# Attention scores as four row-tiled matmuls of 32 partitions, keys spread over 4 copies instead of 16, in a four-layer transformer kernel

## What is computed

```python
s = jnp.einsum('blhd,bmhd->bhlm', q, k)
if causal:
    s = jnp.where(mask, s, -jnp.inf)
p = jax.nn.softmax(s, axis=-1)
return jnp.einsum('bhlm,bmhd->blhd', p, v)
```

## Time and profile before

| | us |
|---|---|
| median of 3 runs | 4222.94 (4222.19 to 4223.15) |
| the profiled execution | 4218.46 |
| its span | 4216.7 |
| TensorE matmuls busy | 4112.9 |
| TensorE weight loads busy | 2922.2 |
| VectorE busy | 2716.3 |
| ScalarE busy | 2733.6 |
| GpSimd busy | 1597.5 |

### The profile page before, as it was taken

How to read it: one execution, slowest core, us unless ns; L and a number is a source line. 1 busy time by engine, 2 the same in 40 slices (tenths; PEclk the granted TensorE clock), 3 DMA queues, 4 the chain that set the end, 5 groups by cost and what they waited for, 6 DMA issues and landing times.

```text
span 4216.7 us, 87546 instructions
## 1 busy us (share of the span) xinstructions
PE 4112.9 (98%) x32576; PEld 2922.2 (69%) x32576; DVE 2716.3 (64%) x5914; ACT 2733.6 (65%) x4850; POOL 1597.5 (38%) x1316
## 2 busy tenths in 40 slices
PE   7999999999999999999999999999999999999998
PEld 4666677776667777777766767777776666777775
DVE  7766555567776655556787765655677776555565
ACT  4677766556667776655666777665566677666555
POOL 4444322234553432124455433223344543321233
PEclk9999999999999999999999999999999999999999
DMA  1000011000000001110000000101000000011000
GB/s 60 1 3 23 13 43 39 33 29 1 17 9 3 23 13 42 41 41 19 10 9 9 3 23 23 43 31 41 19 10 10 9 3 23 24 41 41 31 14 9
DMA packets 52621, 92.60 MB, mean 22 GB/s; under 512 B 11817, under 2 KB 35313, under 8 KB 51953
## 3 DMA queue, kind: packets, MB, share of 16 engines
q1 hardware_dynamic: 52208, 87.01, 6.3%
HBM read 82.80 MB, written 4.19 MB: 21 GB/s over the span
## 4 chain that ended last, share of the span: by engine, by line
PE 87%; DVE 6%; ACT 3%; DMA 1%; POOL 1%; issue 1%; SPq 0%; POOLq 0%; ACTq 0%; DVEq 0%
PE ps L952 19%; PE ps L965 14%; PE ps L1034 11%; PE ps L1042 10%; PE ps L977 8%; PE ps L985 3%; PE ps L926 3%; PE ps L997 2%; PE ps L955 2%; PE ps L935 2%; PE ps L910 2%; PE ps L1002 1%; PE ps L1091 1%; PE ps L1061 1%; DVE mx L1342 1%
## 5 line engine op out<-in xcount | busy, mean ns | idle before, releaser
L1531 POOL TENSOR_TENSOR kx<-kT,k_sb 128x616 f32<-128x616 f32 (+1 forms) x704 | 1038.4, 1475 | 1191.9 <-PE ps L952 621.5
L952 PE MATMUL ps<-kx,qT 128*128 128x308 f32 (+1 forms) x2816 | 1067.7, 488 | 16.4 <-DVE pr L1348 7.1
L1342 DVE TENSOR_REDUCE mx<-ps 128x8 f32<-128x616 f32 (+1 forms) x704 | 671.7, 954 | 603.8 <-PE ps L952 341.5
L1190 ACT ACTIVATE pt<-ps 77x512 f32<-77x512 f32 (+1 forms) x1408 | 776.3, 591 | 268.1 <-PE ps L965 265.3
L1181 ACT ACTIVATE pr<-pr 128x616 f32<-128x616 f32 (+1 forms) x704 | 588.0, 837 | 359.5 <-DVE pr L1348 354.7
L965 PE MATMUL ps<-k_sb,pr 128*77 128x128 f32 (+1 forms) x5632 | 783.9, 277 | 2.4 <-ACT og L1199 1.5
L965 PEld LDWEIGHTS ps<-k_sb,pr 128*77 128x77 f32 (+1 forms) x5632 | 630.8, 145 | 168.7 <-issue 141.8
L1348 DVE TENSOR_TENSOR pr<-ps,mx 128x616 f32<-128x616 f32 (+1 forms) x704 | 671.5, 954 | 24.2
L952 PEld LDWEIGHTS ps<-kx,qT 128*128 128x128 f32 x2816 | 477.7, 190 | 253.0 <-issue 174.9
L1034 PE MATMUL ps<-hT,ew 128*128 128x512 f32 x1024 | 452.4, 594 | 3.7 <-DMA ew<-weights 3.6
L977 PE MATMUL ps<-pt,v 77*16 77x128 f32 (+2 forms) x11264 | 428.5, 275 | 2.7 <-ACT pt L1190 2.7
(11 more groups left out here) (168 smaller groups left out, 5076.9 us busy)
## 6 DMA issues: line engine op xcount, KB each, us to landing
ew<-weights SPq DMA_DIRECT2D x128, 512.0 KB, 4.7
x<-x SPq DMA_DIRECT2D x16, 256.0 KB, 3.2
out<-xh SPq DMA_DIRECT2D x16, 256.0 KB, 2.4
cT<-ctx_cols SPq DMA_DIRECT2D x16, 154.0 KB, 3.2
qT<-mask_pairs SPq DMA_DIRECT2D x16, 154.0 KB, 3.3
kx<-ctx_rows SPq DMA_DIRECT2D x16, 154.0 KB
w_sb<-weights SPq DMA_DIRECT2D x1, 1542.0 KB, 7.5
w_sb<-weights SPq DMA_DIRECT2D x1, 1280.0 KB
```

The lines of the kernel that those rows point to most:

```text
L952: i = mm(o, qT[s][:, b * L:(b + 1) * L], k[:, 4 * j * keys:4 * (j + 1) * keys], start=True, stop=mask is None)
L1190: go_act(pt[s][0:keys, q % 2, :], p[0:keys, :], ACT.Copy).then_inc(probsT_ready.sem, 1)
L1342: link(v_.tensor_reduce(m, tile, AX.X, ALU.max, negate=True))
L1531: tell(pool, g_.tensor_tensor(dst, kT[s][:, b * keys:(b + 1) * keys].unsqueeze(1).broadcast_to([128, 8, keys]), masks.unsqueeze(2).broadca ...
```

## The change

- `scores` becomes one step for a whole batch. It writes `heads // 4` banks: four row tiles of 32 partitions for 16 heads, two of 64 partitions for 8 heads. Tile `g` contracts only its own 32 (or 64) partitions, which hold heads 4g to 4g+3. The masks are put into the banks first.
- `spread` becomes one step for a batch with 4 copies of the keys: copy `j` keeps, in each group, the rows of head `j` of that group (`in_tile`, two small reductions made once). `kx` has four slots of `4 * keys` columns per stream in the same memory.
- The softmax is a step of its own, `soft`, once per half, and each half releases its own pair of banks.
- The planner: costs in `parts` changed for nearly all steps, `LATE` (a delay after TensorE and ScalarE) added, `HOP` from 0.15 to 0.1, another choice among free banks, any adjacent pair instead of four fixed ones, and new values of `LEAD`, `PHASES`, `STAY` and `EAGER`. So the order of every queue differs.

```diff
-            out += [("spread", a, s, *units[n]), ("scores", a, s, *units[n])]
+            if not units[n][1]:
+                out += [("spread", a, s, units[n][0]), ("scores", a, s, units[n][0])]
+            out.append(("soft", a, s, *units[n]))
...
     if kind == "scores":
-        mask = 0.0 if t.mask is None else 0.3 + 0.0034 * keys
-        return [(P, pe(4 * keys, 2) + mask), (V, 2.55 if t.own else 1.7), (A, act(8 * keys))]
+        tiles = t.heads // 4
+        mask = 0.0 if t.mask is None else tiles * (0.02 + 0.0004 * 4 * keys)
+        return [(P, 0.3 + (0.00182 if tiles == 4 else 0.00182) * 4 * keys + mask)]
+    if kind == "soft":
+        return [(V, 2.52 if t.own else 1.67), (A, act(8 * keys, 0.5))]
...
-            option = min(banks_of(step), key=lambda o: max(bank_free[b] for b in o))
-            clear = max(bank_free[b] for b in option)
-            if clear == FOREVER:
+            free_now = [bank_free[b] + HOP <= t for b in range(8)] + [False]
+
+            def cost(o):
+                clear = max(bank_free[b] for b in o)
+                beside = sum(free_now[b - 1] + free_now[b + 1] for b in o)
+                return max(clear + HOP, t), beside, -sum(bank_free[b] for b in o)
+            option = min(banks_of(step), key=cost)
+            if max(bank_free[b] for b in option) == FOREVER:
                 return None
-            t = max(t, clear + HOP)
+            t = cost(option)[0]
...
-LEAD = 2.64378649
-PHASES = (0, 0.270197968, 0.113519094, 0.191236723)
-STAY = 60.9002828
...
+LEAD = 0.416394515
+PHASES = (0, 0.280901424, 0.477195298, 0.528231786)
+STAY = 47.9352789
...
-ANY = [(b,) for b in (7, 6, 5, 4, 3, 2, 1, 0)]
-BANKS = {"scores": [(0, 1), (2, 3), (4, 5), (6, 7)], "rope": [(4, 5), (6, 7), (0, 1), (2, 3)]}
...
+ONE = [(b,) for b in range(8)]
+TWO = [(b, b + 1) for b in range(7)]
+FOUR = [a + b for a in TWO for b in TWO if a[1] < b[0] or b[1] < a[0]]
...
+        if step[0] == "soft" and engine == V:
+            pair = 2 * step[4]
+            bank_free.update(dict.fromkeys(banks["scores", *step[1:4]][pair:pair + 2], end))
...
-                    for j in range(2):
-                        o = bank(pl, step, j)[:, 0:4 * keys]
-                        i = mm(o, qT[s][:, b * L:(b + 1) * L], k[:, 4 * j * keys:4 * (j + 1) * keys],
-                               start=True, stop=mask is None)
-                        if mask is not None:
-                            i = mm(o.rearrange("p (h k) -> p h k", h=4), ident16,
-                                   mask.unsqueeze(1).broadcast_to([128, 4, keys]), start=False, stop=True)
+                    tiles = t.heads // 4
+                    outs = [bank(pl, step, g)[:, 0:4 * keys] for g in range(tiles)]
+                    if mask is not None:
+                        for o in outs:
+                            mm(o.rearrange("p (h k) -> p h k", h=4), ident16,
+                               mask.unsqueeze(1).broadcast_to([128, 4, keys]), start=True, stop=False)
+                    high = 128 // tiles
+                    for g, o in enumerate(outs):
+                        r = slice(high * g, high * (g + 1))
+                        i = mm(o, qT[s][r, b * L:(b + 1) * L], spread_keys[s][r, pl.slot(("spread", a, s, b), NB), 0:4 * keys],
+                               start=mask is None, stop=True)
...
+                link(nc.vector.tensor_reduce(in_tile[heads], K(f"heads{heads}").rearrange("p (g j) -> p j g", j=4), AX.X,
+                                             ALU.add))
...
-                    dst = kx[s][:, pl.slot(step, 2), 0:8 * keys].rearrange("p (h k) -> p h k", h=8)
-                    masks = K("heads16")[:, 8 * h:8 * h + 8] if t.heads == 16 else K("heads8")
                     tell(pool, g_.tensor_tensor(
-                        dst, kT[s][:, b * keys:(b + 1) * keys].unsqueeze(1).broadcast_to([128, 8, keys]),
-                        masks.unsqueeze(2).broadcast_to([128, 8, keys]), ALU.mult), keys_spread, *args)
+                        spread_keys[s][:, pl.slot(step, NB), 0:4 * keys].rearrange("p (h k) -> p h k", h=4),
+                        kT[s][:, b * keys:(b + 1) * keys].unsqueeze(1).broadcast_to([128, 4, keys]),
+                        in_tile[t.heads].unsqueeze(2).broadcast_to([128, 4, keys]), ALU.mult), keys_spread, *args)
```

More of the change, by code:

```diff
@@ L200, in act @@
 def act(n, bias=0.0):
-    return 0.165 + 0.00086 * n + 0.1 * bias
+    return 0.06 + 0.00082 * n + 0.1 * bias
 def parts(step):
     kind, n = step[0], NB * L
-    if kind in ("project", "rope", "values", "spread", "scores", "turn", "mix", "regroup", "out"):
+    if kind in ("project", "rope", "values", "spread", "scores", "soft", "turn", "mix", "regroup", "out"):
         t = ATT[step[1]]
@@ L290, in inputs_of @@
     kind, args = step[0], step[1:]
-    if kind in ("project", "rope", "values", "bias", "spread", "scores", "turn", "mix", "regroup", "out"):
+    if kind in ("project", "rope", "values", "bias", "spread", "scores", "soft", "turn", "mix", "regroup", "out"):
         a, s = args[:2]
@@ L304, in inputs_of @@
         if a and of == "k":
-            out.append((parts(step)[1][0], ("spread", a - 1, s, *last), None))
+            out.append((parts(step)[1][0], ("spread", a - 1, s, NB - 1), None))
         if a and of == "v":
@@ L327, in inputs_of @@
     if kind == "spread":
+        return [(None, (t.project, a, s, "k"), None)]
+    if kind == "scores":
+        return [(None, ("spread", *args), None), (None, (t.project, a, s, "q"), None)]
+    if kind == "soft":
         n = units.index(args[2:])
[L329 to L333, removed]
+        return ([(None, ("scores", *args[:3]), None)]
                 + ([(V, ("turn", a, s, units[n - 2][0], 2 * units[n - 2][1] + 1), P)] if n >= 2 else []))
@@ L354, in inputs_of @@
     if kind == "context":
-        return [(None, ("scores", 2, s, NB - 1, ATT[2].halves - 1), P)]
+        return [(None, ("scores", 2, s, NB - 1), P)]
     if kind == "fetch":
@@ L426, in ready @@
                 return None
[L427 removed]
+            t = ends[step, chain[k - 1][0]] + LATE[chain[k - 1][0]] + HOP
         else:
@@ L436, in ready @@
                     continue
-                end = ends.get((other, theirs or parts(other)[-1][0]))
-                if end is None:
+                by = theirs or parts(other)[-1][0]
+                if (other, by) not in ends:
                     return None
-                t = max(t, end + HOP)
+                t = max(t, ends[other, by] + LATE[by] + HOP)
         return t
@@ L492, in timetable @@
         if k and chain[k - 1][0] == P and step in banks:
-            bank_free.update(dict.fromkeys(banks[step], end))
+            bank_free.update(dict.fromkeys(banks[step], end + LATE[engine]))
+        if step[0] == "soft" and engine == V:
+            pair = 2 * step[4]
+            bank_free.update(dict.fromkeys(banks["scores", *step[1:4]][pair:pair + 2], end))
         for which, (first, final) in enumerate(SHARED):
@@ L505 @@
 FOREVER = 1e9
-LEAD = 2.64378649
-PHASES = (0, 0.270197968, 0.113519094, 0.191236723)
-STAY = 60.9002828
[L509 to L512, removed]
-ANY = [(b,) for b in (7, 6, 5, 4, 3, 2, 1, 0)]
-BANKS = {"scores": [(0, 1), (2, 3), (4, 5), (6, 7)], "rope": [(4, 5), (6, 7), (0, 1), (2, 3)]}
+LEAD = 0.416394515
+PHASES = (0, 0.280901424, 0.477195298, 0.528231786)
+STAY = 47.9352789
+EAGER = {"load": 1.5, "stats": -0.3, "apply": -0.2, "bias": -4, "spread": 2.7, "scores": 0.3,
+         "bias_mlp": -0.2, "hidden": 0.4, "context": 4.1, "fetch": -4.6, "down": -0.1, "step_size": 16.4,
+         "step_size2": -8.8, "decay_in": -1.8, "decay": 2.6, "weigh": 3.8, "gate_stats": -0.2,
+         "gate_norm": -10.3, "mamba_out": -0.3, "final": -3.9, "store": -3.7}
 WITH_PSUM = ("turn", "mix", "regroup", "norm", "values", "project", "turn_out", "out", "hidden", "mlp", "route", "gates",
@@ L517 @@
              "mamba_out")
+ONE = [(b,) for b in range(8)]
+TWO = [(b, b + 1) for b in range(7)]
+FOUR = [a + b for a in TWO for b in TWO if a[1] < b[0] or b[1] < a[0]]
 def banks_of(step):
-    return BANKS.get(step[0]) or (ANY if step[0] in WITH_PSUM else None)
+    if step[0] == "scores":
+        return FOUR if ATT[step[1]].heads == 16 else TWO
+    return TWO if step[0] == "rope" else ONE if step[0] in WITH_PSUM else None
 class Plan:
@@ L542, in __init__ @@
                 self.before[step] = list(dict.fromkeys(last[b] for b in self.banks[step] if b in last))
-                last.update(dict.fromkeys(self.banks[step], step))
+                for n, b in enumerate(self.banks[step]):
+                    last[b] = ("soft", *step[1:], n // 2) if step[0] == "scores" else step
         self.rank, self.sames = {}, {}
@@ L546, in __init__ @@
             for step in steps:
-                if step[0] in ("spread", "scores", "mix"):
+                if step[0] in ("spread", "soft", "mix"):
                     same = self.sames.setdefault((step[0], step[2] % S), [])
@@ L780, in build @@
```

(2 more changed lines are left out.)

95 lines of the change are left out of this document (49 added, 46 removed).

## The result

The changed kernel takes 4012.92 us (median, 4011.71 to 4015.95) against 4222.74: a ratio of 0.9504, 95% interval 0.9488 to 0.9521. It is 5% faster, and 273 us slower than the forecast of 3740, outside the range of 3600 to 3900. Its profiled execution took 4011.71 us, against 4218.46 before.

A forecast was written before the change was run, and what follows sets the result against it. The prediction took TensorE, busy for 4112.9 of 4216.7 us, as the bound. From 4218.5 us it took 548 for faster score matmuls and added 70 of stalls: 3740 us, range 3600 to 3900.

The forecast's parts named there:

- the term of 548 us: Score matmuls on TensorE: four row tiles run at once, steps of 1.16 and 0.82 us, saving 548 us.
- the extra 0.30: Per score step: 0.20 us for entering and leaving tiled mode, about 0.10 for the first of four loads not overlapped.
- loads one after another: Rival for the score step: row groups load one after another, saving only 404 us, time 3860; chance 0.08.
- staggered pairs: Rival for the score step: eight matmuls need five slots instead of two, saving 255 us, time 3964; chance 0.05.
- no overlap: Rival for the score step: row tiles don't overlap, switching adds 77 us, time 4295, slower; chance 0.05.
- the lighter GpSimd: Spreading on GpSimd falls from 1038 to about 294 us, beside TensorE; no gain booked.
- The stalls that come: Attention-heavy stretches: VectorE holds 87% at most, 65 us of stalls, plus 5 for banks and order: 70 us.
- 74% is all that is shown over 400 us: Argument for the binding engines rival: the trace shows VectorE at most 74% busy over 400 us.
- The rival of binding engines: Attention-heavy stretches: VectorE, ScalarE and banks hold each other up at 80% of VectorE, 215 us, time 3885; chance 0.15.
- The step on the softmax halves: Softmax: scores of both halves hold four banks, second pair 2.45 us longer; mid-size pressure, shown as TensorE idle.
- Its sign of being wrong: On TensorE: idle time over 250 us with waits for the shifted scores (banks) or for ScalarE's copies.

The follow-up runs named there:

- untiled: The changed kernel with each score matmul contracting all 128 partitions instead of its own row tile, order of all queues unchanged: 4466.65 us.
- halves_s: The changed kernel with scores by halves again, two row tiles of 32 partitions into two banks per 8 heads, and its own priorities: 4021.19 us.
- hold: The changed kernel with each half's two banks released only after ScalarE's exponential instead of VectorE's add, order planned anew: 4234.11 us.
- oldparams: The changed kernel with the earlier values of LEAD, PHASES, STAY and EAGER, all steps, costs and bank choice as changed: 4175.18 us.

## Why the prediction was wrong

Right, nearly to the digit, was the term of 548 us. Four at a time, read off the column-tiled mix, held for row tiles; the step with its entry is 1.07 + 0.09 = 1.16 us and 0.74 + 0.09 = 0.83 us, forecast 1.16 and 0.82. Of the extra 0.30, 0.10 us is the second burst's late start: it comes 0.533 us after the first (median of all steps), where untiled matmuls of 512 columns come 0.430 apart. The prediction had that size, but put it on the first of four loads. The rivals of loads one after another, of staggered pairs and of no overlap are all refuted; the four loads start together, so what the Trainium skill says of a load's length (TensorE: Matmul & The Clock Gate, LDWEIGHTS) agrees with the trace (184 ns for 32 rows, 190 for 128) and yet doesn't set the step's length. The Trainium skill's other page (TensorEngine Tiling (Array Packing), Gotcha 1: PSUM Pressure) says that row tiling raises the pressure on PSUM, as different row tiles write to different banks; the trace agrees that the pressure rose, from 17 to 177 us of waits for banks. The prediction used the same page for the drain alone and priced banks and order at 5 us.

Right too: GpSimd (879.0 us, forecast near 850; 318.9 of it the spreading, forecast 294) and VectorE's busy time. That nothing is gained by the lighter GpSimd wasn't tested; before, TensorE waited for its `kx` for 0.8 us in all.

Wrong was the step **The stalls that come**. It measured the new limit by how full VectorE would be in the attention-heavy stretches, 87 to 90%, and gave 5 us to banks and order together. In place of that term of 70 us, 342 came: 160 us more of visible waits for banks, 52 more of other visible idle time, about 48 by the clock and about 80 hidden. The clock, which the prediction had at 1.00 throughout, was in no term of it. The order is mixed into all of these: with nothing changed but priorities the time is 61 us less or 162 more, and the best run of all, with another list and another search, is 3933 us, still above the range. VectorE is busy for 281.7 of the 400 us from 2000 to 2400:

```profile
2000.00:2400.00 400.00, 360.33 (x3464) 247.66 (x3463) 281.67 (x564) 284.27 (x518) 84.63 (x101) 0.98 0.08 24
```

TensorE is still 10% idle there, and VectorE's fullest 400 us have 302.6, 76%. They had 305.8 before: the prediction's "74% is all that is shown over 400 us" missed that stretch. The rival of binding engines named the banks beside VectorE and ScalarE, but priced them by VectorE alone and stopped at 3885. The step on the softmax halves had a good part of the cause (both halves hold four banks, the second 2.45 us longer), called it mid-size and left it 5 us. Its sign of being wrong, TensorE idle over 250 us with waits for the shifted scores, came true at 316.

The method failed in one point: before, TensorE was so full that hardly a wait of it could be seen (17 us for banks), and nothing in that trace gave the banks a price; the prediction should have given them a wide one. The same order with slower score steps shows the effect: in `untiled` TensorE is busier and waits 127 us for banks, in the changed kernel 177.

Open: how much of the hidden 80 us is bank and how much data, what the clock costs by itself (no run held the clock), and how the 342 us divide between banks and order, as each run that changed the hold and let the planner know has another order too.

## What to carry to other kernels

Before pricing a faster step on the busiest engine, add up how long each scarce buffer is held per step and in how many pieces it is taken; a step that is three times faster and takes twice the banks can give a good part of it back. Where the order of all queues is fixed ahead, a relief is to be measured with an order planned for it: 704 releases a microsecond earlier were worth 16 us in the old order and 53 in one planned for them, and that order without the early releases cost 95. A TensorE wait that ends with an instruction whose output the waiting step never reads was here a wait for a bank.

## What was not expected of the hardware

The halving of the clock: with TensorE's idle time up from 104 to 316 us in many small pieces, the mean granted clock fell from 0.998 to 0.978. Over the runs it goes loosely with the idle time: 0.992 with 141 us in `halves_s`, 0.966 with 451 in `hold`, 0.959 with 421 in `oldparams`. Two row tiles take as long as four (1.06 and 1.07 us). And the second burst of a tiled step comes late, the more so the more columns a load has: by 11 ns in the mix with 16 columns a load (0.120 us after the first, the later ones 0.109 apart), by 24 with 32, by 103 in the scores with 128. Why, no run shows: in the step above the second four loads end 0.22 us before their matmuls start.
